# Probabilities of graphs 2 and 3 turned to features from ScalarE's queue instead of SyncE's

## The reference, cut to what matters

```python
q, k, v = x @ Wq + bq, x @ Wk + bk, x @ Wv + bv          # per graph, 8 heads of 64
scores = einsum('bqhd,bkhd->bhqk', q, k) / sqrt(64) + mask
out    = einsum('bhqk,bkhd->bqhd', softmax(scores), v)
x = layernorm(x + out @ Wo + bo)      # layer 0
x = layernorm(x + out)                # layer 1 (no Wo)
```

## Time and profile before

| | |
|---|---|
| median of three runs | 2954.68 us |
| profiled execution, whole time | 2955.14 us |
| its span, first to last instruction | 2953.3 us |
| PE busy | 2934.7 us (99%) |
| PE weight loads busy | 2474.4 us (84%) |
| DVE busy | 1799.6 us (61%) |
| ACT busy | 1494.8 us (51%) |
| POOL busy | 1364.8 us (46%) |
| mean granted PE clock | 0.998 |
| DMA, mean | 141 GB/s |

### The profile page before, as it was taken

The page is one execution under the profiler, slowest core; times in us unless marked ns, Lnnn a source line. Parts: engine busy times, 40 slices in busy tenths (PEclk is TensorE's granted clock), DMA queues, the critical chain, the costliest instruction groups (busy, mean ns, idle before and its releaser), DMA issues.

```text
span 2953.3 us, 58080 instructions
## 1 busy us (share of the span) xinstructions
PE 2934.7 (99%) x18982; PEld 2474.4 (84%) x18982; DVE 1799.6 (61%) x7061; ACT 1494.8 (51%) x5011; POOL 1364.8 (46%) x1288
## 2 busy tenths in 40 slices
PE   9999999999999999999999999999999999999997
PEld 8888888888888888888888888888888888888886
DVE  4555656565655656465655766666666666666667
ACT  5545454444545454444545455555555555555554
POOL 3454554545454555555454533434344334344434
PEclk9999999999999999999999999999999999999999
DMA  6454434444454444444455545565555565555566
GB/s 195 110 145 111 133 110 135 117 123 136 109 147 111 132 109 135 119 121 137 108 142 143 145 130 160 162 171 161 144 149 161 160 171 155 147 150 162 161 171 172
DMA packets 412575, 417.70 MB, mean 141 GB/s; under 512 B 46144, under 2 KB 310592, under 8 KB 412224
## 3 DMA queue, kind: packets, MB, share of 16 engines
q1 hardware_dynamic: 407280, 410.84, 49.9%
q10 hardware_dynamic: 4992, 3.15, 0.4%
HBM read 145.37 MB, written 103.81 MB: 84 GB/s over the span
## 4 chain that ended last, share of the span: by engine, by line
PE 99%; issue 1%; POOL 0%; DVE 0%; POOLq 0%; DVEq 0%
PE ring L439 47%; PE ring L447 35%; PE ring L471 8%; PE ring L482 8%; PE ring L417 0%; PE ring L607 0%; POOL norm L1038 0%; POOL prob L1025 0%; POOL k_all L1033 0%; POOL x_res L1033 0%; DVE turned L825 0%; PE ring L553 0%; POOLq L36 0%; DVE prob L825 0%; DVE x_bias L849 0%
## 5 line engine op out<-in xcount | busy, mean ns | idle before, releaser
L1025 POOL TENSOR_TENSOR prob<-prob,inv_sum 128x512 f32<-128x512 f32 x512 | 537.0, 1075 | 730.5 <-DVE inv_sum L813 730.5
L658 ACT ACTIVATE prob<-prob,neg_max 128x128 f32<-128x128 f32 x2048 | 791.6, 392 | 101.1 <-DVE neg_max L805 101.1
L805 DVE CUSTOM_DVE_ANT_0 prob<-ring,mask 128x128 f32<-128x128 f32 x2048 | 440.9, 286 | 525.0 <-PE ring L471 524.8
L638 ACT ACTIVATE k_all<-ring,bk_col 128x512 f32<-128x512 f32 x256 | 310.5, 1216 | 677.1 <-PE ring L439 677.1
L645 ACT ACTIVATE q_all<-ring,bq_col 128x512 f32<-128x512 f32 x256 | 176.7, 690 | 483.9 <-PE ring L439 483.9
L447 PE MATMUL ring<-w_hi_v,xt_hi 128*128 128x512 f32 x1024 | 406.4, 397 | 0.0
L447 PE MATMUL ring<-w_hi_v,xt_lo 128*128 128x512 f32 x1024 | 398.9, 390 | 0.0
L447 PE MATMUL ring<-w_lo_v,xt_hi 128*128 128x512 f32 x1024 | 398.6, 389 | 0.0
L439 PE MATMUL ring<-xt_lo,w_hi_q 128*128 128x512 f32 x1024 | 398.3, 389 | 0.0
L439 PE MATMUL ring<-xt_hi,w_hi_q 128*128 128x512 f32 x1024 | 398.3, 389 | 0.0
L439 PE MATMUL ring<-xt_hi,w_lo_q 128*128 128x512 f32 x1024 | 398.3, 389 | 0.0
(11 more groups left out here) (92 smaller groups left out, 4655.7 us busy)
## 6 DMA issues: line engine op xcount, KB each, us to landing
prob_t<-turned SPq DMA_DIRECT2D x1016, 128.0 KB, 2.7
x_res<-x_tok SPq DMA_DIRECT2D x252, 256.0 KB, 3.7
x_raw<-x_feat SPq DMA_DIRECT2D x196, 256.0 KB, 3.0
x_feat<-x_turned SPq DMA_DIRECT2D x512, 64.0 KB, 2.2
x_tok<-x_bias SPq DMA_DIRECT2D x128, 256.0 KB, 2.3
at_lo<-x_bias SPq DMA_DIRECT2D x244, 64.0 KB, 2.1
out<-x_bias SPq DMA_DIRECT2D x61, 256.0 KB, 4.2
out<-x_turned SPq DMA_DIRECT2D x61, 256.0 KB, 4.0
```

The costliest lines, as they stand in the source:

```text
L638: act.activation(k_all[:, m, :].rearrange("p (b j n) -> p b n j", b=QB, n=SQ), ring[key_bank(s, m)][:].rearrange("p (b n j) -> p b n j", b ...
L658: last = act.activation(prob[b][:, i, n, :], prob[b][:, i, n, :], ACT.Exp, bias=neg_max[b][:, i, n:n + 1], scale=-1.0, accum_out=row_sum[b ...
L805: last = dve.tensor_tensor_reduce(prob[b][:, i, n, :], score_bank(b, i)[:, n, :], mask[layer][:], -SCALE, BIG, ALU.add, ALU.min, neg_max[b ...
L1025: pool.tensor_tensor(prob[b][:, i], prob[b][:, i], inv_sum[b][:, i, :].unsqueeze(2).to_broadcast([P, NC, NODES]), ALU.mult).then_inc(norm_ ...
```

## The change

SP keeps its turn_probs of graphs 2 and 3 only in the last step. In all other steps ACT has a turn_probs of its own with the same waits and the same four transfers: for graph 2 ahead of the first keys_out, and for graph 3 between the first and the second keys_out.

```diff
@@ SP, step(s)
-                if la is not None:
+                if s == LAST:
                     turn_probs(a, 2)
                 if lf is not None:
                     finished(f, 0)
                     finished(f, 1)
-                if la is not None:
+                if s == LAST:
                     turn_probs(a, 3)
@@ ACT
+            def turn_probs(a, b):
+                need(act, att_done, QB * a + b - 3)
+                act.wait_ge(turned_set, 2 * (QB * a + b) + 2)
+                for n in range(BLK):
+                    act.dma_start(prob_t[b][:, n], turned_of(a, b)[n * SQ:(n + 1) * SQ]).then_inc(prob_t_in[b], 16)
+
             def step(s):
                 a = s - 1
                 lp, la = layer_of(s), layer_of(a)
+                if la is not None:
+                    turn_probs(a, 2)
                 if lp is not None:
                     for m in range(NC):
                         keys_out(s, m)
+                        if la is not None and m == 0:
+                            turn_probs(a, 3)
```

## The result

The changed kernel takes 2966.18 us (median of 7 runs, 2961.29 to 2969.03) against 2954.9 us (7 runs, 2954.62 to 2955.91): a ratio of 1.0037, 95% interval 1.0027 to 1.0046. It is 11.3 us slower, which is clear of the 0.2% that a measurement tells from no change. Another chip gave 2965.66 against 2954.87 us, 1.0038 (1.0024 to 1.0052). The time lies inside the stated range of 2952.5 to 2967, but only because that range was drawn up into the slower rival's small gaps. It is the time of that rival, which had a chance of 0.17, and not that of the forecast, 2955.0 with no gap; it lies outside the forecast's own range, which ended at 2959. The profiled execution took 2968.45 us, 13.3 more than that of before.

What follows compares the result with a forecast made beforehand. PE was taken as the bound, busy 2934.7 of 2953.3 us. The profiled 2955.14 us plus 0.3 for a few single steps, less 0.46 to the median, gave 2955.0; range 2952.5 to 2967.

Steps and rivals of the forecast that it cites:

- the slower rival: Layer 1: ACT's key copies come after PE wants them, a gap recurring in 29 steps; 2969.5 us at 0.5 each; chance 0.17.
- PE is the bound, nothing to win: Steady steps: PE has no gap another engine could close, so freeing about 5 us a step on SP is worth 0.
- Layer 0 costs nothing: Layer 0 steps: keys ready at 1030.6 against 1039.07 wanted, over 8 us to spare; cost 0.
- The place, the waiting instruction and the deadline in layer 1: Layer 1: key copies behind graph 3's issue must end before values(s, 0), where `k_set` stands, at 2389.11; 2.70 us early.
- ACT's own issue of graph 3 ... I take 3.2, +0.7: Layer 1, ACT's queue: four transfers of graph 3 take 3.2 us instead of 2.49, costing 0.7 of the slack.
- No gap opens; cost 0: Layer 1: delays of 1.6 us fit into 2.70 in the step shown and 2.2 in the worst, so PE never waits.
- The 4.68 of the earlier trace: Layer 1, kernel before: SP once needed 4.68 us for graph 3's four issues; taken as upper end, +2.2.
- Delay of the turn, 0.6 + 0.3: Layer 1: graph 3's turn waits for graph 1's carry, put back 0.6 us by overlapping issues and 0.3 by data.
- The rival's price: Layer 1, key copies late for PE: a gap of 0.5 us in each of 29 steps, 14.5 us; chance 0.17.
- a slack of 2.7 with 1.6 of it spent on guesses: Layer 1: keys 2.70 us early in the step shown, less assumed delays of 1.6, leaving 1.1.
- Signs of being wrong: PE waiting for `k_all`, layer 1 steps over 40.29 us, graph 3's turn under 6.3 before values(s, 0), four ACT issues over 4.
- The fourth: Layer 1: graph 3's turn ending less than 6.3 us ahead of values(s, 0) would show the forecast wrong.

Runs made afterwards that it cites:

- behind_keys: The changed kernel with ACT's issue of graph 3 behind the fourth key copy instead of the first; 2955.15 us, ratio 1.0 against the kernel before.
- only2: The kernel before with only graph 2's transfers moved to ACT's queue, graph 3's staying on SP's; 2955.13 against 2955.12 us.
- held: The changed kernel, but in layer 1 SP waits until graph 3 has landed before stores and residual loads of graphs 0 and 1; 2955.05 us.

## Why the prediction was wrong about the likeliest case

- **PE is the bound, nothing to win: right.** Taking up to 5 us a step off SP's queue made no kernel faster.
- **Layer 0 costs nothing: right.** PE is busy for all of its stretch.
- **The place, the waiting instruction and the deadline in layer 1: right.** Key copies behind the issue of graph 3, `k_set` ahead of values(s, 0); behind_keys takes them from behind it and the loss is gone.
- **"ACT's own issue of graph 3 ... I take 3.2, +0.7": the step that failed.** It measured 4.51, +2.0, so that "No gap opens; cost 0" became 17 gaps in 29 steps. I took a value between the two rows of the last step (2.98 and 3.99), and these come from transfers of 64 KB in another phase. The nearest rows for this place were SP's, and SP was alone. The 4.68 of the earlier trace rows, which I had as the upper end, is about what the mean step looks like with two queues.
- **Delay of the turn, 0.6 + 0.3: near.** 0.71 measured. In only2, where graph 2's part stands by itself, it was 0.5 of issuing and 0.2 of data.
- **Small terms left out.** ACT takes 0.1 from its last issue to the first copy, and key copies must end 3.0 us ahead of the scores, not 2.72 (2389.11 to 2391.83): some 0.4 together.
- **The sum.** From the mean turn: 11.26 - 0.71 - 4.51 - 3.1 - 0.1 leaves 2.84 where 3.0 is needed. With 3.2 in place of 4.51 it would have left 4.15. I set one price for each delay against the slack; but the issue alone ran from 3.58 to 5.36, only the late steps pay and the others give nothing back, so a mean overrun of 0.2 becomes 0.44 us a step, 12.8 us in 29.
- **The rival's price** of 0.5 us a step and its deciding point, the three delays passing the slack together, were right; its chance of 0.17 was too low for a slack of 2.7 with 1.6 of it spent on guesses. That the range held the time is owed to this rival's 0.4 us a step and not to the forecast; the upper end of 2967 is 0.8 above the median, and two of the seven runs, 2968.45 and 2969.03, lie beyond it.
- **Signs of being wrong.** Three of the four came: PE waiting for `k_all`, longer steps, and over 4 us for four issues. The fourth did not: the turn never ended less than 7.0 us ahead of values(s, 0). Its 6.3 was 3.2 + 3.1 and held the same mis-sized issue, so it would have missed every gap here.

## What to carry to other kernels

A transfer issued on ACT's queue held up ACT for the whole issue, 2.60 to 4.51 us on the mean for four, and with it everything behind it in program order. Put such an issue behind the copies with the nearest deadline, and size it by an issue with both queues at work, not by the same issue on a queue that was alone. Where several delays share one slack, test them together: here each half of the change measured as free. And set the slack against the scatter of the delays, not against one value.

## What the runs showed of the hardware

- Four issues of 128 KB from ACT: 2.60 us on the mean with SP standing, 3.07 with SP issuing small loads and whole stores beside it, 4.51 with SP issuing 256 KB transfers; a single issue took up to 2.83 us. SP's own grow beside it: over layer 1 a store took 0.82 us on the mean and a residual load 0.71, against 0.61 and 0.48 before. The two that took 1.31 and 1.93 in step 42 took this in a step of held:

```profile
1784.97 0.45 SPq L251 DMA_DIRECT2D out<-x_turned  x1
1785.51 0.39 SPq L297 DMA_DIRECT2D x_res<-x_tok  x1
```

- The changed kernel's runs spread by 7.7 us, those of before by 1.3: once a step depends on how long issues take and when transfers land, their scatter can show in the time. No run tests this by itself.
